# Layer 1 of a graph network: the edge matrix by transposes, the index list copied at the group's start, weights in PSUM, the next scores between the adds

## What is computed

```python
s_u = x @ W_u.T + b_u                     # 8 heads
s_v = x @ W_v.T
e = leaky_relu(s_u[src] + s_v[dst], 0.2)
m = segment_max(e, dst)
e_exp = exp(e - m[dst])
denom = segment_sum(e_exp, dst)
msg = x.reshape(n, 32, 8)[src] * (e_exp / denom[dst])[:, None, :]
out = segment_sum(msg, dst)
```

## Time and profile before

| | |
|---|---|
| median of three runs | 4935.61 us |
| profiled execution | 4929.81 us |
| its span | 4928.1 us |
| PE, busy | 3099.3 us (63%) |
| VectorE (DVE), busy | 2202.6 us (45%) |
| ScalarE (ACT), busy | 908.4 us (18%) |
| POOL, busy | 3434.9 us (70%) |
| granted TensorE clock, mean | 0.800 |

### The profile page before, as it was taken

How to read it: one execution, slowest core, us unless ns; L and a number is a source line. 1 busy time by engine, 2 the same in 40 slices (tenths; PEclk the granted TensorE clock), 3 DMA queues, 4 the chain that set the end, 5 groups by cost and what they waited for, 6 DMA issues and landing times. The chain is left out here.

```text
span 4928.1 us, 61408 instructions
## 1 busy us (share of the span) xinstructions
PE 3099.3 (63%) x13554; PEld 1900.6 (39%) x13555; DVE 2202.6 (45%) x5019; ACT 908.4 (18%) x2810; POOL 3434.9 (70%) x2948
## 2 busy tenths in 40 slices
PE   3547877777777777877778768834444444444441
PEld 1224444444444444444444435523333333333331
DVE  2543333333333333333333349855555555555554
ACT  0212222222222222222222223300000000000002
POOL 4238888888888888888888867756666666666564
PEclk9869898888998888888898889956666666666665
DMA  7777767667767677677677666643333333333332
GB/s 285 193 241 137 135 126 136 133 123 135 132 126 138 127 131 134 126 135 132 123 136 132 123 133 206 181 148 93 95 92 100 93 94 91 96 98 94 92 93 66
DMA packets 471760, 641.52 MB, mean 130 GB/s; under 512 B 173608, under 2 KB 365636, under 8 KB 467887
## 3 DMA queue, kind: packets, MB, share of 16 engines
q0 software_dynamic: 198144, 339.26, 36.4%
q1 hardware_dynamic: 245994, 254.83, 17.6%
q10 hardware_dynamic: 27588, 47.08, 3.0%
HBM read 448.23 MB, written 192.71 MB: 130 GB/s over the span
## 5 line engine op out<-in xcount | busy, mean ns | idle before, releaser
L935 POOL DMA_INDIRECT S<-l_msum,l_sink x784 | 1280.7, 1634 | 254.2 <-issue 213.5
L1466 POOL DMA_INDIRECT l_feats<-X_rows,l_gsrc x880 | 1008.1, 1146 | 605.6 <-DVE l_gsrc L1574 340.7
L918 POOL DMA_INDIRECT l_ga<-A_rows,l_gsrc x784 | 791.3, 1009 | 265.6 <-issue 155.4
L1008 PE MATMUL l_psU<-l_hid,l_same 128*128 128x257 f32 x1568 | 585.0, 458 | 534.7 <-ACT l_hid L1044 518.2
L981 PE MATMUL l_psC<-l_table,l_onehot 128*128 x4728 | 726.5, 295 | 0.0
L1532 PE MATMUL l_psU<-l_feats,l_same 128*128 128x264 f32 x1760 | 555.7, 481 | 146.5 <-DVE l_feats L1699 129.2
L1048 ACT COPY l_msum<-l_psU 128x257 f32<-128x257 f32 x784 | 292.6, 373 | 1883.8 <-POOLq L934 1296.1
L974 PE MATMUL l_psC<-W1cT,l_attrT 64*128 64x256 f32 x1576 | 619.0, 476 | 13.1 <-DMA l_table<-B_rows 13.1
L981 PEld LDWEIGHTS l_psC<-l_table,l_onehot 128*128 128x128 bf16 x4728 | 426.0, 104 | 364.9 <-issue 303.4
L1008 PEld LDWEIGHTS l_psU<-l_hid,l_same 128*128 128x128 f32 x1568 | 266.1, 213 | 669.9 <-ACT l_hid L1044 598.9
L1532 PEld LDWEIGHTS l_psU<-l_feats,l_same 128*128 128x128 f32 x1760 | 413.8, 242 | 281.8 <-issue 189.2
(11 more groups left out here) (346 smaller groups left out, 3512.2 us busy)
## 6 DMA issues: line engine op xcount, KB each, us to landing
l_srcb<-src_rows SPq DMA_DIRECT2D x99, 512.0 KB
l_locb<-lo_rows SPq DMA_DIRECT2D x55, 512.0 KB
S<-su_zeros ACTq DMA_DIRECT2D x24, 1156.5 KB
l_locb<-loc_rows SPq DMA_DIRECT2D x99, 256.0 KB
nd_sums<-S SPq DMA_DIRECT2D x196, 128.5 KB, 2.2
l_attr<-in_edge_attr SPq DMA_DIRECT2D x98, 256.0 KB
GH_rows<-l_hidden SPq DMA_DIRECT2D x49, 384.0 KB
nd_hidden<-GH_rows SPq DMA_DIRECT2D x49, 384.0 KB, 3.2
```

Of the source, the lines that this page charges most:

```text
L918: pool.indirect_dma_start(ga[:, s, :], None, D["A"], bass.IndirectOffsetOnAxis(ap=gsrc[h][:, j % HALF:j % HALF + 1], axis=0)).then_inc(gat ...
L935: pool.indirect_dma_start(D[f"S{j % NTAB}"], bass.IndirectOffsetOnAxis(ap=sink[j // HALF][:, j % HALF:j % HALF + 1], axis=0), msum[:, j % ...
L1008: nc.tensor.matmul(psU[j % 2][:, 0:UW], same[j // HALF][:, j % HALF, :], hid[:, j % RING, :], start=True, stop=True).then_inc(agg_done, 1)
L1466: pool.indirect_dma_start(feats[r][:, t, :], None, D["X1"], bass.IndirectOffsetOnAxis(ap=gsrc[r][:, t:t + 1], axis=0)).then_inc(gathered[r ...
```

## The change

1. `find_edge` goes. TensorE transposes `onehot` tile by tile with a bf16 identity into a PSUM bank `psS`, eight tiles at a time (`turn_nodes`), and ScalarE copies each half as float32 into `same` (`keep_edges`), which now has two sets. VectorE waits for the transposes of group g before it writes `onehot` for group g + 1.
2. `stage_index(g + 2)` moves from the end of VectorE's body to its start.
3. ScalarE writes the weights twice: first into 128 free columns of the bank `psV`, from which VectorE reads them while it multiplies, then into `feats`, from which TensorE sums the denominators.
4. The last four adds are split: `take_scores(g + 1)`, adds 4 and 5, `local_max(g + 1)`, adds 6 and 7. TensorE turns the scores between pair 5 and pair 6.

```diff
+            def turn_nodes(g, half):
+                if not isinstance(g, int) or g or half:
+                    pe.wait_ge(same_ready, 2 * g + half)
+                for t in range(HALF):
+                    i = nc.tensor.transpose(psS[:, t, :], onehot[:, half * HALF + t, :], identb[:, :])
+                i.then_inc(same_turned, 1)
...
                 if not last:
                     dst_scores(g + 1, 1 - r, 1)
+                    turn_nodes(g + 1, 0)
                 pe.wait_ge(max_ready, g + 1)
...
-                pe.wait_ge(same_ready, g + 1)
+                pe.wait_ge(same_ready, 2 * g + 2)
+                pe.wait_ge(weights_in_rows, g + 1)
...
+                    if n == 2 and not last:
+                        turn_nodes(g + 1, 1)
+                    if n == 5 and not last:
+                        turn_scores(g + 1, 1 - r)
                 if not last:
-                    turn_scores(g + 1, 1 - r)
                     gather_ends(g + 1)
...
+            def keep_edges(g, r, half):
+
+                act.wait_ge(same_turned, 2 * g + half + 1)
+                if not isinstance(g, int) or g >= SETS:
+                    act.wait_ge(agg_done, (g - SETS + 1) * PAIRS)
+                    act.sem_inc(act_waited, 1)
+                nc.scalar.copy(same[r][:, half * HALF:(half + 1) * HALF, :], psS[:, :, :]).then_inc(same_ready, 1)
...
                 nc.scalar.activation(shrink[:, :], psE[:, SHRINK:SHRINK + NH], ACT.Exp).then_inc(shrink_ready, 1)
+                if not last:
+                    keep_edges(g + 1, 1 - r, 0)
                 act.wait_ge(below_ready, g + 1)
-                nc.scalar.activation(feats[r][:, :, H:XW], below[:, :, :], ACT.Exp).then_inc(weights_ready, 1)
+                nc.scalar.activation(weight, below[:, :, :], ACT.Exp).then_inc(weights_ready, 1)
+                nc.scalar.activation(feats[r][:, :, H:XW], below[:, :, :], ACT.Exp).then_inc(weights_in_rows, 1)
+                if not last:
+                    keep_edges(g + 1, 1 - r, 1)
...
+                if not isinstance(g, int) or g < XG - SETS:
+                    stage_index(g + SETS, r)
                 if not last:
+                    dve.wait_ge(same_turned, 2 * g + 2)
                     find_node(g + 1, 1 - r)
...
-                if not first:
-                    dve.wait_ge(agg_done, g * PAIRS)
-                find_edge(g)
...
-                    w3 = f[:, :, H:XW].unsqueeze(2).to_broadcast([P, QUARTER, H // NH, NH])
+                    w3 = weight[:, q * QUARTER:(q + 1) * QUARTER, :].unsqueeze(2).to_broadcast([P, QUARTER, H // NH, NH])
...
-                add_sums(g, (4, 5, 6, 7), blocks)
                 if not last:
                     take_scores(g + 1, 1 - r, c)
+                add_sums(g, (4, 5), blocks)
+                if not last:
                     local_max(g + 1, 1 - r, c)
-                if not isinstance(g, int) or g < XG - SETS:
-                    stage_index(g + SETS, r)
+                add_sums(g, (6, 7), blocks)
```

More of the change, by code:

```diff
@@ L1353, in layer1_phase @@
         onehot = m.sb("onehot", [P, GROUP, P], BF16)
-        same = m.sb("same", [P, GROUP, P])
+        same = [m.sb(f"same{r}", [P, GROUP, P]) for r in range(SETS)]
+        identb = m.sb("identb", [P, P], BF16)
         svrest = m.sb("svrest", [P, NB, NH])
@@ L1509, in _ @@
             dst_scores(0, 0, 1)
+            turn_nodes(0, 0)
+            turn_nodes(0, 1)
             turn_scores(0, 0)
@@ L1531, in body @@
                     for t in range(n * PAIR, (n + 1) * PAIR):
-                        i = nc.tensor.matmul(psU[n % 4][:, 0:XW], same[:, t, :], feats[r][:, t, :],
+                        i = nc.tensor.matmul(psU[n % 4][:, 0:XW], same[r][:, t, :], feats[r][:, t, :],
                                              start=(t % PAIR == 0), stop=(t % PAIR == PAIR - 1))
                     i.then_inc(agg_done, 1)
+                    if n == 2 and not last:
+                        turn_nodes(g + 1, 1)
+                    if n == 5 and not last:
+                        turn_scores(g + 1, 1 - r)
                 if not last:
-                    turn_scores(g + 1, 1 - r)
                     gather_ends(g + 1)
@@ L1558, in _ @@
                 stage_window(r, r)
+            for half in range(2):
+                keep_edges(0, 0, half)
             def body(g, r, first, last):
@@ L1578, in find_node @@
                 nc.vector.tensor_scalar(onehot[:, :, :], locb[r][:, :, :], K["winid"][:, 0:1], None, ALU.is_equal).then_inc(onehot_ready, 1)
-            def find_edge(g):
-                nc.vector.tensor_tensor(same[:, :, :], K["column"][:, :].unsqueeze(1).to_broadcast([P, GROUP, P]),
-                                        K["loX"][:, bass.ds(g * GROUP, GROUP)].unsqueeze(2).to_broadcast([P, GROUP, P]),
-                                        ALU.is_equal).then_inc(same_ready, 1)
             def take_scores(g, r, c):
```

12 lines of the change are left out of this document (7 added, 5 removed).

## The result

Four runs of the changed kernel took 5065.94 to 5068.61 us (median 5066.81); the kernel before, run beside it, took 4938.36 us. The ratio is 1.0261 [1.0243, 1.0279]: the change made the kernel 128 us **slower**, against a forecast of 385 us faster. The profiled execution took 5065.94 us, with a span of 5064.2 us.

A forecast was written before the change was run, and what follows sets the result against it. The gather's loop of 29.41 us was taken to bound a group; then VectorE's chain would: 23.23 - 0.75 - 0.57 - 0.4 + 0.1 + 0.3 = 21.9 us against 28.97, 382 us saved, 4550 us forecast, range 4475 to 4650 us.

The forecast's parts named there:

- Part 1: POOL's gathers: with the index list copied at the body's start, POOL costs 20.2 or 21.9 us a group and stops bounding.
- VectorE's own chain: VectorE's work and waits from landing to last add, 23.23 us before, forecast to set the cycle at 21.9 us.
- Part 2: Terms on VectorE's chain: find_edge out -0.75, wait for turned scores -0.57, late adds' waits -0.4 us (0 to -0.8).
- VectorE now waits for POOL: slower: Rival: nine instructions after the landing each wait out a 0.94 us gather; chain 30.4 us, kernel 5012 us; chance 0.03.
- Early index list: Start of VectorE's body: the list is ready about a whole group early, leaving POOL only its queue and agg_done.
- What frees POOL: Of 3.4 us excess per 16 gathers, find_edge's removal saves 1.5 us and weights in PSUM perhaps the other 1.9.
- `find_edge` out, transposes in: VectorE gains 0.75 us a group; TensorE's transposes (eight in 1.2 us) and ScalarE's 1.1 us copy cost +0.1 and +0.3.
- the rival of dear transposes: Rival: TensorE transposes cost 0.283 us each, eight 2.26 us; cycle 24.1 us, kernel 4673 us; chance 0.18.
- The clock: Rival: TensorE's clock stays up through the sums, POOL bounds at 20.4 us a group; kernel 4473 us; chance 0.12.
- The wait for the spread carries: VectorE, with find_edge no longer covering the carries' trip through TensorE, would idle about 0.9 us for that product.

The follow-up runs named there:

- e7: The changed kernel with no edit, run again where releases were prompt: 4493.5 us, ratio 0.9166 to the kernel before.
- e3: The changed kernel with the index copy back at the end of VectorE's body, releases prompt: 4885.4 us, ratio 0.9955 to the kernel before.
- e2: The kernel before with only the index copy moved to the start of VectorE's body, releases prompt: 4638.9 us, ratio 0.9453.
- e4: The changed kernel with VectorE's comparison back in place of the transposes and ScalarE's copies, releases prompt: 4532.1 us, ratio 0.9236.
- e16: The changed kernel with a POOL fill and a wait for it added before each four gathers, releases held up: 4702.0 us, ratio 0.9524.
- e17: The changed kernel with VectorE's comparison back and the weights read from SBUF, releases held up: 4733.1 us, ratio 0.9587.
- e1: The changed kernel with POOL waiting for VectorE's adds, not TensorE's pairs, releases prompt: 4487.2 us, ratio 0.9146.
- e12: The changed kernel with the index copy back at the end of VectorE's body, releases held up: 5083.1 us, ratio 1.0296.
- e14: The changed kernel with VectorE's comparison back in place of transposes and copies, releases held up: 4920.1 us, ratio 0.9963.

## Why the prediction was wrong

**The step that failed** is the one sentence on which Part 1 ends: "So POOL leaves the path, and VectorE's own chain becomes the cycle." POOL did leave the path as an engine. But VectorE's chain waits for TensorE at the scores, at the carries, at the turned maxima and at the adds, and I priced all these waits by the earlier trace rows. In the condition of the result a release by TensorE under an unbroken train can come 2 to 10 us late, where the earlier trace rows show at most 0.5, and a group became 31.26 us and not 21.9. The term that was most mis-sized is the one for the adds in Part 2, -0.4 us: against e7 their waits grew by 6.9 us a group; the first use of the carries and the subtraction added 2.0 together.

Why didn't show it is in part argued. There the turned scores and the segments' ends fall in the 3.90 us in which POOL stood idle after the landing, and the carries beside a comparison that stretched a gather to 2.44 us; the turned maxima end 1.06 us after that gather, and the subtraction follows them by 0.43 us. The change takes away both the idle stretch and the stretching. The warning could have been had from the trace before: the setup rows above are its own, with 1.98 us from a matmul's end to its waiter under the same train. I had read layer 1 alone.

The rival "VectorE now waits for POOL: slower" (5012 us, 3 in 100) had sign and size, by another mechanism. Its price was that instructions wait out a gather; but they run at full speed (the weighted multiplication has a mean of 1.215 us in both conditions), and what is late is the release of those that wait for TensorE. Its condition, "with gathers all the time they share it", was the right place to look.

**The other steps, read in e7**, where releases are prompt, and the forecast of 4550 us meets 4493.5 us, from a kernel before at 4904.4 us: a gain of 411 us for 382. That is inside the stated range, but below the 4510 to 4600 us that I gave the forecast itself:

- *Early index list.* Right where releases are prompt. Late, the same kernel takes 4885.4 us (e3), so this part carries 392 of the 411 us; alone it brings 268 us (e2), because POOL then bounds at 16 x (1.186 + 0.30) = 23.8 us against a measured (4530.2 - 3236.4)/54 = 23.96 us. I had said 23.2 us.
- *What frees POOL.* Right in both terms. From e4 to e7 the comparison goes: (1.048 - 0.955) x 16 = 1.5 us, as said. From e2 to e4 the weights move to PSUM: (1.186 - 1.048) x 16 = 2.2 us, where I had 1.9. My totals didn't quite follow from these terms (19.8 us without both, where I wrote 20.2, and 21.7 with the second, where I wrote 21.9); e7's gathers need (0.956 + 0.30) x 16 = 20.1 us. The Trainium skill (SBUF — State Buffer, Who interferes with whom) says that a VectorE instruction contends with a GpSimd instruction that reads SBUF when two of its inputs lie there, and not with one; the gathers agree, at 0.955 us beside a multiplication with one.
- *`find_edge` out, transposes in.* Forecast 0.75 - 0.1 - 0.3 = 0.35 us a group; measured (4532.1 - 4493.5)/54 = 0.7 us. The transposes were mis-sized: eight take 1.01 us at a granted clock of 0.50 and 0.61 at 1.00, not 1.2. The copy took 1.012 us, not 1.1. The exponential followed the subtraction at once (4033.96 + 0.29 to 4034.28), 0.38 us after the copy: the cover was as thin as I thought. So the rival of dear transposes is out; each record says 0.31 us, but eight overlap. The Trainium skill's 275 ns (TensorE: Matmul & The Clock Gate, part 4) is that record's size, and not the cost in a row of eight.
- *The clock.* In e7 it was 1.00 until 4030, fell to 0.50 by 4031 and stayed there through the first two pairs, and was 1.00 again from 4041. It falls later than in the kernel before, where it is 0.50 from the landing on, but the first pairs still run at 0.50, so that rival is out too.
- *VectorE's own chain.* 21.31 us for 21.9. The wait for the spread carries was 1.11 us, for 0.9.

So there is no single answer to whether the change is faster: it is 8.3% faster or 2.6% slower, by a condition that the kernel doesn't set. One version was seen to beat the kernel before in both: the early index list alone (4639 and 4696 us), by 5.5% and 4.9%. e16 and e17 beat it where releases are held up (4702 and 4733 us) and were not run where they are prompt. There e1 is the lowest, at 4487 us, but its 6 us to e7 are within the intervals.

## What to carry to other kernels

Before an ablation is believed, run the changed kernel itself beside the ablations, and look at what the control took: here four unrelated edits "cured" a delay that was simply absent when they ran. When idle time is put down to a releaser that makes no sense, compare the end of the true producer with the start of its waiter, and do so in every phase of the trace before, not only in the one that changes. And a stream of DMAs issued by POOL back to back may not be free for the others, even when every instruction beside it keeps its length: price each wait for TensorE under it, and try an order that leaves it a gap where the short chains run. A gap elsewhere doesn't help (e12).

## What the hardware showed that I had not expected

- Releases by TensorE reached VectorE and ScalarE 2.6, 8.3 and over 10 us late while POOL gathered every 1.25 us, and what was still held came through 2 to 3 us after the last gather's end, with every instruction's own duration unchanged. Releases by VectorE reached TensorE within 0.07 us in the same groups. In the setup, with the same spacing, TensorE's were 0.6 to 2.7 us late each.
- The condition belongs to the occasion: one program, 4491 to 4502 us or 5057 to 5069 us, and nothing between; each of the two spreads is under 0.3%.
- Adding work to the busiest queue gained 358 us (e16), and making each gather 0.12 us dearer gained 187 us (e17 against e14), both where releases are held up.
- Eight bf16 transposes of 128x128 in a row take 1.01 us at a granted clock of 0.50 (1.2 GHz) and 0.61 us at 1.00 (2.4 GHz), though the record of one is 0.22 to 0.32 us long.
